# Expert steps written out, a third buffer for first-layer weights, and the last 64 hidden rows stacked high over low

## The reference, cut to what matters

```python
# x: 4096 tokens x 256, after a layernorm; 9 experts, hidden width 704, top 2
scores = sigmoid(x_flat @ gate.T + bias)
top_scores, selected = top_k(scores, 2)
top_scores = top_scores / (sum(top_scores, -1) + 1e-20)
cw = einsum('tk,tke->te', top_scores, one_hot(selected, 9))
for e in range(9):
    h = silu(x_flat @ ew1[e].T) * (x_flat @ ew3[e].T)     # 704 wide
    out = out + cw[:, e:e + 1] * (h @ ew2[e].T)           # back to 256
x = x + tanh(g_ffn) * out
```

## Time and profile before

| | us |
|---|---|
| median of 3 runs | 1065.64 |
| lowest and highest | 1060.14, 1067.1 |
| the profiled execution | 1068.61 |
| its span, first to last instruction | 1066.3 |

### The profile page before, as it was taken

One profiled execution on the slowest core, in us unless ns is written; L12 is line 12 of the kernel. 1 busy time (PEld: TensorE's weight loads), 2 busy tenths in 40 slices (PEclk: granted clock), 3 DMA queues, 4 the chain that ended last, 5 costly groups with the idle time before them and its releaser, 6 DMA issues.

```text
span 1066.3 us, 19701 instructions
## 1 busy us (share of the span) xinstructions
PE 847.0 (79%) x5990; PEld 642.0 (60%) x5990; DVE 634.1 (59%) x1715; ACT 424.3 (40%) x960; POOL 393.4 (37%) x403
## 2 busy tenths in 40 slices
PE   5994976958577877753267999989898999989895
PEld 5993343524334443432166778878686878878784
DVE  5223599596877869594794555545454545545452
ACT  3222665556464646452001434433332433433341
POOL 1000456354443626262002244434534344433533
PEclk9999975567575656565555999999898999999998
DMA  5631475463626354442141487776778686776872
GB/s 165 195 117 31 155 236 174 152 200 133 207 101 223 122 186 166 147 152 87 31 167 31 137 242 231 242 232 210 237 232 247 196 248 208 238 223 206 255 225 56
DMA packets 90796, 187.79 MB, mean 176 GB/s; under 512 B 14176, under 2 KB 51552, under 8 KB 90720
## 3 DMA queue, kind: packets, MB, share of 16 engines
q1 hardware_dynamic: 51408, 135.48, 38.4%
q10 hardware_dynamic: 25488, 32.90, 8.7%
q0 software_dynamic: 13824, 18.43, 8.0%
HBM read 145.10 MB, written 42.73 MB: 176 GB/s over the span
## 4 chain that ended last, share of the span: by engine, by line
PE 36%; DMA 7%; DVE 5%; issue 4%; POOL 2%; ACT 1%; SPq 1%; DVEq 0%; POOLq 0%; ACTq 0%
PE bank L997 32%; DMA w<-w_d 6%; PE bank L907 3%; PE bank L991 1%; POOL out L979 1%; DVE xl L1051 1%; DMA out<-res,sid 1%; DVE topi L806 0%; SPq L946 0%; PE bank L759 0%; DVE hlo L1084 0%; DMA w_d<-whl 0%; POOL xg L969 0%; DVE hf L1097 0%; ACT hh L1062 0%
## 5 line engine op out<-in xcount | busy, mean ns | idle before, releaser
L997 PE MATMUL bank<-xh,w 128*128 128x256 bf16 (+1 forms) x1760 | 282.6, 271 | 27.8 <-DMA w<-w_d 16.0
L997 PE MATMUL bank<-xl,w 128*128 128x256 bf16 (+1 forms) x880 | 229.3, 270 | 0.0
L997 PEld LDWEIGHTS bank<-xh,w 128*128 128x128 bf16 x1760 | 170.1, 101 | 58.6 <-issue 27.4
L1068 ACT ACTIVATE sg<-bank 128x256 f32<-128x256 f32 (+1 forms) x240 | 86.6, 361 | 284.4 <-PE bank L997 284.4
L1095 DVE TENSOR_TENSOR hf<-sg,bank 128x256 f32<-128x256 f32 (+1 forms) x200 | 78.8, 394 | 152.2 <-ACT sg L1068 151.8
L979 POOL DMA_INDIRECT out<-res,sid x72 | 116.7, 1621 | 120.5 <-DVE res L1109 88.1
L997 PE MATMUL bank<-w,hh 128*128 128x256 bf16 (+1 forms) x864 | 150.1, 273 | 0.0
L591 POOL TENSOR_TENSOR whl<-wst,whl 128x1224 bf16<-128x1224 f32 x32 | 83.4, 2605 | 138.8 <-ACT whl L561 138.8
L487 PE MATMUL bank<-qbd,kvb 128*128 128x512 f32 x128 | 110.3, 958 | 11.7 <-DVE Cm L600 10.6
L997 PE MATMUL bank<-w,hlo 128*128 128x256 bf16 (+1 forms) x432 | 117.5, 272 | 0.0
L1084 DVE TENSOR_TENSOR hlo<-hf,hh 128x256 bf16<-128x256 f32 (+1 forms) x240 | 93.7, 390 | 5.6 <-ACT hh L1062 1.3
(11 more groups left out here) (225 smaller groups left out, 1445.8 us busy)
## 6 DMA issues: line engine op xcount, KB each, us to landing
w<-w_d SPq DMA_DIRECT2D x40, 1408.0 KB, 9.1
w<-w_d SPq DMA_DIRECT2D x40, 768.0 KB
wst<-in_wts SPq DMA_DIRECT2D x32, 612.0 KB, 4.1
w_d<-whl ACTq DMA_DIRECT2D x32, 612.0 KB, 3.4
kvb<-in_kv SPq DMA_DIRECT2D x32, 260.0 KB, 2.7
xa<-in_x SPq DMA_DIRECT2D x8, 512.0 KB, 5.0
ka<-in_kv SPq DMA_DIRECT2D x8, 512.0 KB, 3.7
qT_d<-qt ACTq DMA_DIRECT2D x8, 512.0 KB, 3.0
```

The source lines that it names most:

```text
L997: mm = nc.tensor.matmul(dst, l, r, start=(n == 0), stop=(n == len(pairs) - 1))
L1068: nc.scalar.activation(sg[m % 2][0:K, 0:N], bank[0:K, 2 + (NM * w + m) % 4, 0:N], ACT.Silu).then_inc(f_sg, 1)
```

## The change

Four things are changed together.

1. The loops over steps are gone on PE, ACT, DVE and POOL: all 40 steps are written out, and their waits compare with constants. SP keeps a loop, over six steps.
2. `w13` has three buffers (`W3`), with a semaphore each. SP's order becomes: `w13` of steps 0 and 1, then for each s `w2_` of s and `w13` of s+2. The load of `w13` for step s waits for the first layer of s-3, not of s-2. To make room, buffers of the matrix-LSTM and of the weight conversion lie under those of stages three and four; `r_dve` therefore first waits for the last store to `w_d`.
3. `TG` and `TS` are int32 from the start, and the indirect DMAs read their row numbers straight from them. The casts into `gid` and `sid`, with a wait for each, are gone.
4. For m = 5 the low half is written under the high half, on partitions 64 to 127 of `hh`, and the host lays the last 64 rows of w2 twice into the weights, in place of zeros. Two 128-row matmuls (stack by high weights, stack by low weights) take the place of three 64-row ones; they add one small product, low by low.

```diff
+W3 = 3
...
-        TG = sb("TG", [P, NQ]); TS = sb("TS", [P, NQ]); TE = sb("TE", [P, STEPS, NE]); tA = sb("tA", [P, NQ])
+        TG = sb("TG", [P, NQ], I32); TS = sb("TS", [P, NQ], I32); TE = sb("TE", [P, STEPS, NE]); tA = sb("tA", [P, NQ])
...
+            for w in range(2):
+                dve.wait_ge(w_out[w], 16 * NT // 2)
             dve.wait_ge(c_lg, NB)
...
-        w13 = [sb(f"w13_{w}", [P, 2, W13], BF16) for w in range(2)]
+        w13 = [sb(f"w13_{w}", [P, 2, W13], BF16) for w in range(W3)]
...
-        def f_sync(sp, s, w):
+        def f_w1_sync(sp, s, w):
             e = sp.value_load(eoff[0:1, bass.ds(s, 1)], min_val=0, max_val=(NE - 1) * WE)
-            ge(sp, f_l1, s * NM - NM)
+            ge(sp, f_l1, (s - 2) * NM)
             sp.dma_start(w13[w][:, :, :], w_d[:, :, bass.ds(e, W13)]).then_inc(f_w1[w], 16)
+
+        def f_w2_sync(sp, s, w):
+            e = sp.value_load(eoff[0:1, bass.ds(s, 1)], min_val=0, max_val=(NE - 1) * WE)
             ge(sp, f_y, s - 1)
             sp.dma_start(w2_[w][:, :, :], w_d[:, :, bass.ds(e + W13, W2C)]).then_inc(f_w2[w], 16)
...
-            nc.gpsimd.tensor_copy(gid[w][:, 0:nj], TG[:, bass.ds(column(i, m), nj)]).then_inc(f_gid, 1)
-            ge(pool, f_gid, s + 1)
-            for j in range(nj):
+            for j in range(tiles(s)):
+                c0 = column(s) + j
                 nc.gpsimd.indirect_dma_start(xg[w][:, j, :], None, y_d,
-                                             bass.IndirectOffsetOnAxis(ap=gid[w][:, j:j + 1], axis=0)).then_inc(f_xg[w], 16)
...
-            ge(pool, f_out, rows_up_to(i, m - 1))
-            nc.gpsimd.tensor_copy(sid[w][:, 0:nj], TS[:, bass.ds(column(i, m), nj)]).then_inc(f_sid, 1)
-            ge(pool, f_sid, s + 1)
+            ge(pool, f_out, landed(s - 1))
             ge(pool, f_res, s + 1)
...
                 for m in range(NM):
-                    K = P if m < NM - 1 else HREM
                     c0 = m * D
-                    hi, lo = hh[w][0:K, m, j * P:(j + 1) * P], hl_[w][0:K, m, j * P:(j + 1) * P]
-                    wh, wl = w2_[w][0:K, 0, c0:c0 + D], w2_[w][0:K, 1, c0:c0 + D]
-                    pairs += [(hi, wh), (hi, wl), (lo, wh)]
+                    hi = hh[w][:, m, j * P:(j + 1) * P]
+                    wh, wl = w2_[w][:, 0, c0:c0 + D], w2_[w][:, 1, c0:c0 + D]
+                    pairs += [(hi, wh), (hi, wl)]
+                    if m < NM - 1:
+                        pairs.append((hl_[w][:, m, j * P:(j + 1) * P], wh))
...
-                V.tensor_tensor(hl_[w][0:K, m, 0:N], hf[m % 3][0:K, 0:N], hh[w][0:K, m, 0:N], ALU.subtract).then_inc(f_hl, 1)
+                if m < NM - 1:
+                    V.tensor_tensor(hl_[w][:, m, 0:N], hf[m % 3][:, 0:N], hh[w][:, m, 0:N], ALU.subtract).then_inc(f_hl, 1)
+                else:
+                    V.tensor_tensor(hh[w][HREM:P, m, 0:N], hf[m % 3][0:HREM, 0:N], hh[w][0:HREM, m, 0:N],
+                                    ALU.subtract).then_inc(f_hl, 1)
...
+            f_w1_sync(sp, 0, 0)
+            f_w1_sync(sp, 1, 1)
             for s in range(4):
-                f_sync(sp, s, s % 2)
-            with sp.Fori(2, STEPS // 2) as i:
-                for w in range(2):
-                    f_sync(sp, i * 2 + w, w)
+                f_w2_sync(sp, s, s % 2)
+                f_w1_sync(sp, s + 2, (s + 2) % W3)
+            with sp.Fori(0, (STEPS - 4) // 6 - 1) as i:
+                for u in range(6):
+                    f_w2_sync(sp, i * 6 + (u + 4), u % 2)
+                    f_w1_sync(sp, i * 6 + (u + 6), u % W3)
...
-            slots(pe, f_pe)
-            f_l2_pe(pe, LASTB, BODY - 1)
+            for s in range(STEPS):
+                f_l1_pe(pe, s)
+                if s + 1 < STEPS:
+                    f_T_pe(pe, s + 1)
+                if s:
+                    f_l2_pe(pe, s - 1)
+            f_l2_pe(pe, STEPS - 1)
...
-    w2 = np.concatenate([w2, np.zeros((NE, NM * P - HID, D), np.float32)], 1)
+    w2 = np.concatenate([w2, w2[:, full:]], 1)
```

More of the change, by code:

```diff
@@ L50 @@
 STEPS = FULL + HALF
-BODY = 2 * GRP
 NQ = 2 * FULL + HALF
+W3 = 3
 YW = D + 16
@@ L962, in f_gather, with landed @@
-        def f_gather(pool, i, m):
-            s, w, nj = i * BODY + m, m % 2, tiles(m)
+        tiles = lambda s: 1 if s % GRP == GRP - 1 else 2
+        column = lambda s: (s // GRP) * (2 * GRP - 1) + 2 * (s % GRP)
+        def landed(s, w=None):
+            return sum(16 * tiles(k) for k in range(s + 1) if w in (None, k % 2))
+        def f_gather(pool, s):
+            w = s % 2
             ge(pool, f_T, s - 1)
             ge(pool, f_cwt, s - 1)
-            nc.gpsimd.tensor_copy(gid[w][:, 0:nj], TG[:, bass.ds(column(i, m), nj)]).then_inc(f_gid, 1)
-            ge(pool, f_gid, s + 1)
-            for j in range(nj):
+            for j in range(tiles(s)):
+                c0 = column(s) + j
@@ L977, in f_scatter @@
+        def f_scatter(pool, s):
+            w = s % 2
+            ge(pool, f_out, landed(s - 1))
             ge(pool, f_res, s + 1)
-            for j in range(nj):
-                nc.gpsimd.indirect_dma_start(out, bass.IndirectOffsetOnAxis(ap=sid[w][:, j:j + 1], axis=0),
+            for j in range(tiles(s)):
+                c0 = column(s) + j
+                nc.gpsimd.indirect_dma_start(out, bass.IndirectOffsetOnAxis(ap=TS[:, c0:c0 + 1], axis=0),
                                              res[w][:, j, :], None, bounds_check=TOK - 1, oob_is_err=False,
@@ L983, in build, with f_T_pe @@
         XT = lambda w: bank[:, w, :].rearrange("p (k t) -> p k t", k=KD)
-        def f_T_pe(pe, i, m):
-            s, w = i * BODY + m, m % 2
-            ge(pe, f_xg[w], rows_up_to(i, m, w))
+        def f_T_pe(pe, s):
+            w = s % 2
+            ge(pe, f_xg[w], landed(s, w))
             ge(pe, f_xl, s - 1)
-            for j in range(tiles(m)):
+            for j in range(tiles(s)):
                 for k in range(KD):
@@ L998, in three, with f_l1_pe @@
             return mm
-        def f_l1_pe(pe, i, b):
-            s, w, N = i * BODY + b, b % 2, tiles(b) * P
-            ge(pe, f_w1[w], i * (8 * BODY) + (b // 2) * 16 + 16)
+        def f_l1_pe(pe, s):
+            w, N = s % 2, tiles(s) * P
+            wt = w13[s % W3]
+            ge(pe, f_w1[s % W3], (s // W3) * 16 + 16)
             ge(pe, f_xh, s + 1)
@@ L1101, in f_h_dve, with f_e_dve @@
             lo(NM - 1)
-        def f_e_dve(dve, i, b):
-            s, w, nj = i * BODY + b, b % 2, tiles(b)
+        def f_e_dve(dve, s):
+            w = s % 2
             ge(dve, f_y, s + 1)
             ge(dve, f_cws, s + 1)
-            ge(dve, f_out, rows_up_to(i, b - 2))
-            for j in range(nj):
+            ge(dve, f_out, landed(s - 2))
+            for j in range(tiles(s)):
                 ins = nc.vector.tensor_scalar(res[w][:, j, :], bank[:, 6 + w, j * D:(j + 1) * D], cws[w][:, j:j + 1], None,
@@ L1270, in _ @@
             r_tab_dve(dve)
-            f_x_dve(dve, 0, 0)
-            slots(dve, f_dve)
-            f_e_dve(dve, LASTB, BODY - 1)
+            f_x_dve(dve, 0)
+            for s in range(STEPS):
+                f_h_dve(dve, s)
+                if s + 1 < STEPS:
+                    f_x_dve(dve, s + 1)
+                if s:
+                    f_e_dve(dve, s - 1)
+            f_e_dve(dve, STEPS - 1)
         @block.gpsimd
```

163 lines of the change are left out of this document (61 added, 102 removed).

## The result

The changed kernel takes 1014.76 us (median of 4 runs, 1013.68 to 1015.93), beside 1066.37 us for the kernel before in the same measurement (4 runs, 1060.14 to 1068.68). The ratio is 0.9525, with a 95% interval of 0.9483 to 0.9567. By the medians 51.6 us are saved. The prediction was 1014 us. The profiled execution took 1013.68 us with a span of 1011.9 us; against the 1068.61 and 1066.3 of before that is 54.9 and 54.4 us less, and the sum in the prediction was 53.5.

What follows compares the result with a forecast made beforehand. PE was taken as the bound inside a group, with stops for weights at group starts. Savings of 32.8 + 19.7 + 1.0 = 53.5 us from 1068.6 gave 1015.1; the predicted median was 1014 us, range 1006 to 1034.

Steps and rivals of the forecast that it cites:

- Third buffer: Expert stage, PE at group starts: a third `w13` buffer and SP's new order remove weight stops and slow restarts, 32.8 us.
- Stack: Second layer on PE: one matmul spacing and two height changes saved, 0.31 us per tile, 19.7 us over 32 full steps.
- the half steps give nothing: Eight half steps: the stack saves nothing, as PE already waits 0.46 us for `xl`, growing to some 0.8.
- The write to partitions 64 to 127: DVE's low half written to other partitions: taken as zero cost, 3 us at most behind half steps.
- Casts: POOL: 0.48 us saved at the first gather and 0.5 in the tail, 1.0 us in sum.
- Written-out steps: Expert-stage steps outside loops: no gain of their own; fetching longer code bounded by 0 and +3 us.
- POOL: Next limit, its scatters: 50.9 us per group against PE's 52.1; scatter chain ends at 1003, before PE's 1012.8.
- that slack all but goes: POOL's 88 us of waiting for `res` in 28 scatters was to nearly vanish.
- rival A: POOL bounds mildly, a full scatter taking 10.3 to 10.9 us: 1020 to 1042 us, put at 1027; chance 0.15.
- Rival B: Scatters starve behind weights, a full one taking 12 us: 1083 us, slower than before; chance 0.06.
- 315 GB/s as the engines' room: DMA engines: a group needs 250 GB/s, 0.8 of the 315 seen while weights flowed, so they have time left.

## Why the prediction was right, and where it was not

**Third buffer, 32.8 us.** Right, by the mechanism: no wait of PE for weights after step 2, none of the slow restarts, and 31.8 us when it is taken away again. I had priced it from the trace of before. It was right there by more than its working deserves: from before's trace 2.1 of the 32.8 belong to the loop (0.28 after each of three landings and 1.21 after a fourth; I had named only "about 1 us" of it and put it inside this term), and without the stack the buffer saves only 21.7. With the stack the stops would have grown, and the buffer takes that away too. The terms are not independent, and the sum came out because they were done together.

**Stack, 0.31 us per tile, 19.7 in all.** Right: 19.4 by unstacking. Both parts of the 0.31 are confirmed by themselves, 0.117 for the matmul and 0.186 to 0.195 for the two changes of height. That the half steps give nothing was right as well: the wait for `xl` in their slot grew from 0.46 to 0.79, as forecast. The write to partitions 64 to 127 takes as long as the one to 0 to 63 (0.42 us each), so zero was right.

**Casts, 1.0 us.** Measured 1.6, inside the spread: neither confirmed nor refuted. In the expert stage itself the first gather was issued 1.5 us earlier than before, more than the 0.48 of the forecast; what is over it comes from stages that were not studied.

**Written-out steps, nothing of their own.** Their slots are the same, as forecast, and no slower code shows. But wherever PE waits in the loop, it starts later, and the run of this part alone came out 5.5 us below before, of which 2.1 are explained. In the changed kernel, where nothing is late, this has nothing left to give.

**POOL.** The forecast, POOL near the bound but not at it, was right within 2.0 us. It missed those: I worked out whether the end of the chain of scatters comes before PE's end (1003 against 1012.8), but not whether a gather queued behind a scatter comes before its transposes. POOL holds both, and the second condition is the tighter one: a scatter that waits 6.75 us for landed rows holds the gather behind it. The slack was misjudged too: I had POOL wait for `res` some 1 us in about half of its scatters. It was 21 of 40, but 6.3 us each. Without the casts that wait holds the time to landing as well; with the casts put back, where landing is waited for first, it can be set beside the earlier trace rows:

```profile
POOL out L984 <- DVE res L1119: 48.9, 21, 11.1
```

Of the 88.1 us 48.9 are left, so "that slack all but goes" was too strong. Neither rival A nor B came true at a load beyond this kernel's: with 328 GB/s the time is 3.8 us longer, below A's 1020. Rival B's price was far too high. In that trace scatters of neighbouring full steps start 11.2 and 11.9 us apart and then 8.5, so the lag does not grow; why the last one is shorter isn't shown. My use of 315 GB/s as the engines' room was wrong as well.

**The first two steps.** Of the 54.4 us, 1.5 came from an earlier start of the expert stage, 52.0 from its steps up to the first layer of step 39, and 0.8 from the tail. Of the 52.0, 2.2 were no part of the forecast. The slow restart in steps 0 and 1 cost 4.2 us in the trace of before and 2.1 in that of the changed kernel. The kernels here show 1.6 to 4.6 at that place; no edit touches these steps in a way that I can tie to it, so I count it as chance, which isn't shown. It made up for the 2.0 of the gathers: that the sum came out so near was luck in this part.

**The reference time.** The profiled execution of before, 1068.6, lies at the high end of its runs. The sum was made against it and the median was 3 us lower, which is why 1014 and not 1015.1 was predicted. In the later jobs before's median was 1058.6 to 1063.0, and against these the gain is 44 to 48 us, not 51.6. The time of the changed kernel was predicted well; that of the gain depends on which runs of before stand beside it.

**The chain that ended last** could have misled me here. In the changed kernel it leaves PE several times and goes through scatters:

```profile
712.55 3.73 PE bank L998 x34
...
719.89 8.52 DMA out<-res,TS
...
731.16 7.60 DMA out<-res,TS
...
739.58 4.93 DMA out<-res,TS
...
745.53 7.37 PE bank L998 x66
```

It reads as if POOL were the bound of this group. DVE's timeline at its end says otherwise:

```profile
743.92 0.42 DVE L1089 TENSOR_TENSOR hh<-hf,hh 64x256 bf16<-64x256 f32 x1
744.37 0.18 DVE L1050 TENSOR_TENSOR cwt<-xg,TE 128x18 f32<-128x18 f32 x1
744.58 0.69 DVE L1054 TENSOR_TENSOR xl<-bank,xh 128x512 bf16<-128x512 f32 x1
```

DVE works without a gap up to `xl`, behind the hidden parts of the step; a landing at 744.51 fell just ahead of it and was taken for its releaser. With half the weights POOL hardly waits for landed rows, and the group is still 52.14 us.

## What to carry to other kernels

Price a missing buffer from the time between the starts of neighbouring stages over many repetitions, not from the stops alone, because each stop can bring a slow restart with it; and price it again with every other edit in place, since a shorter stage ahead of a late load only lengthens the stop. Look for matmuls with another number of rows between full ones: stacking a high half on a low half can save the changes as well as a matmul. When an engine that issues DMAs comes near the bound, check each thing queued behind its longest wait, not only whether it ends in time.

## What the runs showed of the hardware that was not expected

- A change between 128-row and 64-row matmuls costs 0.10 us each way, beyond the spacing of 0.11 us; 64 tiles with two changes each made 11.9 us of difference at an equal number of matmuls.
- The same wait, after the same kind of landing, lets PE go 0.05 us later when it compares with a constant in written-out code, 0.33 us later in the loop, and 1.26 us later across the loop's turn (1.74 in the stack-only kernel).
- One core kept up 328 GB/s over 350 us beside a PE that was busy 98% of the time, at a DMA share of 0.94.
- The length of a stop alone does not tell whether the clock falls. In the kernel before, PE stood 2.26 us ahead of step 5, and there was no slow restart. Ahead of step 10 it stood as long (its timeline, then the chain):

```profile
696.16 0.28 PE L997 MATMUL bank<-xh,w 128*128 128x256 bf16 x1 [2.27 <-DMA w<-w_d]
```
```profile
696.16 8.40 PE bank L997 x60
```

There the 60 matmuls took 1.7 us more than the 6.7 of full clock. In the kernel with written-out steps only it is plainer still: after 1.77 us of idle time, at 814.15, the granted clock of the next 3 us was 0.64; after 2.99 us, at 932.34, it was 1.00. What decides stays open.
